# Border between projection and second attention: waiting for stored queries at each chunk's loads, and the first shift's store issued ahead of ones and x

## The reference, cut to what matters

```python
x = _layernorm(x + _L0_attn_ref(x, ...))           # ends with: return out @ proj_w.T + proj_b
x = _layernorm(x + _L0_xattn_ref(x, ctx_1024, ctx_1024, mask, ...))

def _L0_xattn_ref(q, k, v, mask, Wq, bq, Wk, bk, Wv, bv, Wo, bo):
    qh = _split_heads(q @ Wq.T + bq)
    kh = _split_heads(k @ Wk.T + bk)
    vh = _split_heads(v @ Wv.T + bv)
    scores = jnp.einsum('bhqd,bhkd->bhqk', qh, kh) / jnp.sqrt(jnp.float32(HEAD_DIM))
    scores = scores + mask.astype(scores.dtype) * NEG
    weights = jax.nn.softmax(scores, axis=-1)
    attn = jnp.einsum('bhqk,bhkd->bhqd', weights, vh)
```

## Time and profile before

| What | Value |
|---|---|
| Median of 3 runs | 1844.24 us |
| Lowest and highest run | 1839.27 and 1845.89 us |
| The profiled execution: its own time | 1838.95 us |
| The profiled execution: span | 1837.2 us |
| Mean granted TensorE clock | 0.927 of full speed |
| PE busy | 1628.8 us (89%) |
| DVE busy | 1281.4 us (70%) |
| ACT busy | 1010.5 us (55%) |
| POOL busy | 389.3 us (21%) |

### The profile page before, as it was taken

How to read it: one execution, slowest core, us unless ns; L and a number is a source line. 1 busy time by engine, 2 the same in 40 slices (tenths; PEclk the granted TensorE clock), 3 DMA queues, 4 the chain that set the end, 5 groups by cost and what they waited for, 6 DMA issues and landing times. The chain is left out here.

```text
span 1837.2 us, 36172 instructions
## 1 busy us (share of the span) xinstructions
PE 1628.8 (89%) x14816; PEld 1062.8 (58%) x14816; DVE 1281.4 (70%) x2240; ACT 1010.5 (55%) x1727; POOL 389.3 (21%) x265
## 2 busy tenths in 40 slices
PE   7859999999999999999877599869994999999990
PEld 7734444444444444444366455546763888888890
DVE  6978888888888888888178446752333678777744
ACT  5324777777777777777735267844542233333313
POOL 6550000000000000000015001111551355555521
PEclk9967999999999999999989678978996999999995
DMA  7887443433434333440248866223213244444226
GB/s 251 265 229 197 68 67 62 70 65 65 71 62 67 62 62 64 61 69 9 58 137 232 193 101 122 66 88 110 89 39 111 70 95 96 96 95 95 38 24 194
DMA packets 130388, 184.36 MB, mean 100 GB/s; under 512 B 29466, under 2 KB 93736, under 8 KB 129132
## 3 DMA queue, kind: packets, MB, share of 16 engines
q1 hardware_dynamic: 113456, 153.70, 35.5%
q0 software_dynamic: 13440, 22.07, 5.7%
q10 hardware_dynamic: 3328, 6.29, 2.1%
HBM read 115.32 MB, written 70.06 MB: 101 GB/s over the span
## 5 line engine op out<-in xcount | busy, mean ns | idle before, releaser
L719 DVE TENSOR_REDUCE att_row_max<-att_ring 128x2 f32<-128x1024 f32 x512 | 602.5, 1221 | 110.8 <-PE att_ring L785 57.1
L703 ACT ACTIVATE att_w_exp<-att_s_ps 128x512 f32<-128x512 f32 x999 | 536.2, 599 | 219.2 <-PE att_s_ps L832 146.8
L859 PE MATMUL att_a_ps<-att_w_exp,att_v_group 128*32 128x512 f32 x2048 | 272.8, 605 | 0.8 <-ACT att_acc_sb L692 0.6
L818 PE MATMUL att_s_ps<-att_q_stack,att_k_stack 62*128 62x512 f32 x640 | 181.8, 481 | 0.0
L818 PEld LDWEIGHTS att_s_ps<-att_q_stack,att_k_stack 62*128 62x128 f32 x640 | 84.4, 184 | 123.9 <-ACT att_w_exp L703 112.9
L2344 ACT ACTIVATE ex_hid<-ex_h_ps,ex_b 128x512 f32<-128x512 f32 x128 | 87.3, 686 | 118.5 <-DVE ex_h_lo L2399 64.9
L633 POOL COPY att_eyes<-keep_slope_eye 128x384 bf16<-128x384 bf16 x16 | 8.0, 506 | 634.7 <-PE att_s_ps L832 625.1
L2399 DVE TENSOR_TENSOR ex_h_lo<-ex_hid,ex_h_hi 128x512 fp32r<-128x512 f32 x128 | 138.7, 1084 | 4.4
L2294 POOL DMA_INDIRECT x_scr<-ex_y,ex_home x60 | 101.2, 1687 | 177.0 <-DVE ex_y L2389 163.3
L785 PE MATMUL att_ring<-att_k_stack,att_q_stack 60*128 60x512 f32 x640 | 131.5, 451 | 6.3 <-DVE att_att L746 3.2
L832 PE MATMUL att_s_ps<-att_eyes,keep_past_bf 64*128 64x64 bf16 x3738 | 130.7, 193 | 0.0
(11 more groups left out here) (314 smaller groups left out, 3567.6 us busy)
## 6 DMA issues: line engine op xcount, KB each, us to landing
first_w_raw<-ew SPq DMA_DIRECT2D x16, 1024.0 KB, 7.7
att_k_stack<-qk_scr SPq DMA_DIRECT2D x40, 256.0 KB
rows_scr<-att_zeros POOLq DMA_DIRECT2D x8, 1040.0 KB, 21.0
first_rows<-rows_scr SPq DMA_DIRECT2D x16, 520.0 KB, 4.8
qk_scr<-qkv_t_lo SPq DMA_DIRECT2D x14, 512.0 KB, 4.7
qk_scr<-qkv_t_hi SPq DMA_DIRECT2D x14, 512.0 KB, 4.4
keep_k_stack<-qk_scr SPq DMA_DIRECT2D x24, 256.0 KB
att_q_stack<-qk_scr SPq DMA_DIRECT2D x20, 256.0 KB
```

The costliest lines, as they stand in the source:

```text
L703: nc.scalar.activation(w_exp[(STEPS * g.n + st) % SETS][h][:, :], score_bank(v), ACT.Exp).then_inc(exp_done, 1)
L719: nc.vector.tensor_reduce(out, ring[place.slot][:, :, :], AX.X, ALU.max).then_inc(ring_free, 1)
L818: ins = nc.tensor.matmul(score_bank(v), ks[g.buf][rows, c, j, kt * P:(kt + 1) * P], qs[g.buf][rows, j, c * CH:(c + 1) * CH], start=True, s ...
L859: ins = nc.tensor.matmul(a_ps[32 * h:32 * h + 32, :], vg[g.buf][:, kt, h * VW:h * VW + 32], w_exp[(STEPS * g.n + st) % SETS][h][:, :], sta ...
```

## The change

The wait for the stored queries leaves the end of the projection's block. In its place, each load of a stack of queries waits for the stores of its own chunk, on SP and on ACT. DVE waits for all stores before it computes `wo_lo`, in the middle of the second attention's start. The semaphores `q_out` and the tiles `q_hi` and `q_lo` change their place of allocation for this: the semaphores outlive the stage, and the tiles stand behind the others. Apart from that, `move_top(0)` moves ahead of the ones of stacks 2 and 3 and of x1 of chunk 0.

```diff
@@ cross_tiles
-            "stacks": [s.sb(f"q_stack{i}", [P, PAIRS, CH], F32R) for i in range(2)]}
+            "stacks": [s.sb(f"q_stack{i}", [P, PAIRS, CH], F32R) for i in range(2)],
+            "q_out": [s.sem(f"q_out{i}") for i in range(2)]}
@@ stage_self_out
-        q_hi = [s.sb(f"q_hi{i}", [P, CK, CH], F32R) for i in range(2)]
-        q_lo = [s.sb(f"q_lo{i}", [P, CK, CH], F32R) for i in range(2)]
         norm = Norm(nc, s, io["apart"])
...
         wk_hi, wk_lo = [spare[:, i * 2048:(i + 1) * 2048].rearrange("p (c m) -> p c m", c=CK) for i in range(2)]
+
+        q_hi = [s.sb(f"q_hi{i}", [P, CK, CH], F32R) for i in range(2)]
+        q_lo = [s.sb(f"q_lo{i}", [P, CK, CH], F32R) for i in range(2)]
...
-        q_out = [s.sem(f"q_out{i}") for i in range(2)]
+        q_out = pre["q_out"]
...
             for c in range(2):
                 sp.wait_ge(x1_out[c], 16 * CHUNKS // 2)
-                sp.wait_ge(q_out[c], Q_STORES * CHUNKS // 2)
@@ stage_cross, SP
                 if n >= Q_SETS:
                     sp.wait_ge(s_done, H * (n - Q_SETS) + H)
+                sp.wait_ge(q_out[n % 2], Q_STORES * (n // 2 + 1))
                 load_query_side(sp, io, n, 0, qst[n % Q_SETS])
...
             load_stack(2)
+            move_top(0)
             for i in (2, 3):
                 load_ones(sp, io, qst[i], ones_in)
             load_x(0)
-            move_top(0)
             sp.dma_start(bo, io["bo"].partition_broadcast(P)).then_inc(weights_in, 16)
@@ stage_cross, ACT
+                act.wait_ge(q_out[n % 2], Q_STORES * (n // 2 + 1))
                 load_query_side(act, io, n, 1, qst[n % Q_SETS])
@@ stage_cross, DVE
+            for c in range(2):
+                dve.wait_ge(q_out[c], Q_STORES * CHUNKS // 2)
             dve.wait_ge(hi_done, 1)
             nc.vector.tensor_tensor(wo_lo[:, :, :], wo_raw, wo_hi[:, :, :].bitcast(F32), ALU.subtract).then_inc(lo_done, 1)
```

More of the change, by code:

```diff
@@ L1546, in stage_cross @@
         x2_done = s.sem("x2_done")
-        ones_in = lent["ones_in"]
+        ones_in, q_out = lent["ones_in"], pre["q_out"]
         out_done = s.sem("out_done")
```

## The result

| | Before | Changed |
|---|---|---|
| Median | 1843.20 us (20 runs) | 1834.88 us (20 runs) |
| Lowest and highest run | 1837.82 and 1857.50 us | 1830.36 and 1848.78 us |
| Profiled execution, own time / span | 1838.95 / 1837.2 us | 1835.53 / 1833.7 us |

The ratio of the changed kernel to the one before is 0.9955, with a 95% interval of 0.9938 to 0.9972: 8.3 us less, between 5.2 and 11.4. The forecast was 1834.8 us. The move is real, and its middle is just inside the half per cent.

A forecast was written before the change was run, and what follows sets the result against it. Two PE stalls at the border, 5.20 us (last query store landing) and 5.94 us (shift rows' load), were taken as the bound. Both parts -10.1, ones +0.7, sum -9.4: 1844.24 to 1834.8 us, range 1829.0 to 1841.0.

The forecast's parts named there:

- The border's wait: End of the projection: without the wait for stored queries the new stage begins at 1024.5 instead of 1029.14, 4.6 us saved.
- The added waits: SP and ACT at each stack load, DVE before wo_lo: stores will have landed by then, cost 0.
- The shift's store: First shift store, moved ahead: lands in 2.6 us instead of 8.1, PE's stall before first scores shrinks from 5.94 to 0.45.
- The ones: Ones moved behind the shift: PE waits 0.7 us for them at half 16, bounds no wait and 2.5 us.
- The second part of the change: Shift's store moved ahead of ones and x1: 5.5 us gained at chunk 0's first scores, 0.7 us lost at half 16.
- The sum: Whole kernel: -10.1 + 0.7 = -9.4 us, from 1844.24 to 1834.8 us.
- S: Issue time of the first shift's loads on SP: 1048.19 before, forecast at 1038.05 after the change.
- the cover of the second shift store: Chunk 1's first scores come 27.2 us after S, so a late second shift store is covered by some 5 us.
- Rival 1: Only the border is saved: shift's store still lands in 6.1 to 8.1 us, 1837.6 to 1839.6 us; chance 21%.
- rival 2: Something else holds the border's barrier until about 1029; only 4.8 us saved, 1839.4 us; chance 4%.
- Rival 3: Clock luck: the low-clock stretch in chunk 2 goes, -14.0 us, 1830.2 us; chance 14%.
- rival 4: Clock stays low in chunks 1 to 3: up to 14.8 us lost, +5.4, 1849.6 us; chance 5%.

The follow-up runs named there:

- e7: Changed kernel with SP waiting until all ones are in before it issues x1; one run, no median, PE's wait at half 16 was 4.09 us.
- e3: Changed kernel with the four ones issued ahead of the stack of chunk 2; 1835.32 us, ratio 0.9968 to the kernel before.
- e2: Kernel before with only the new order on SP, the old wait at the border kept; 1838.51 us, ratio 0.9983.
- g1: Kernel before with only the query tiles q_hi and q_lo allocated last; 1842.95 us, ratio 0.9997.
- g2: Repeat of g1, the kernel before with only q_hi and q_lo allocated last; one run, no median.
- f5: Changed kernel with chunk 2's two ones issued between the first shift's store and its wait, the other two later; 1832.21 us, ratio 0.9952 to the kernel before.
- f6: f5 with x1 of chunk 0 and bo moved behind chunk 1's shift; 1832.76 us, ratio 0.9961 to the kernel before.
- e1: Changed kernel with the old order on SP, ones and x1 ahead of the first shift's store; 1836.76 us, ratio 0.9973 to the kernel before.
- f7: Changed kernel with all four ones issued between the first shift's store and the wait for it; one run, no median, A + C 44.2 us.

## Why the prediction was right

**The border's wait** was forecast at 4.6 us. In the two profiles it is 5.23 - 0.56 = 4.7. Over all profiles that wait there A is 6.1 us in the mean (five of them), 0.56 in each that does not: 5.5 us. The profile I worked from had a short landing.

**The added waits** cost nothing, as forecast. DVE's `wo_lo` starts at 1037.70 in the changed kernel, between the maxima of halves 13 and 14 as before, and all query stores had landed at 1027.44. In the profile with the latest landing, e7, it was still 7 us ahead of `wo_lo` (1036.60 and 1043.76).

**The shift's store** was forecast to land in 2.6 us and did. First scores were to come 17.65 us after the first maxima, and came after 17.44 and 17.84. PE's wait was to be 0.45 us and is 0.25 and 0.66. The mechanism of that step was half wrong all the same: I took x1's common landing as the sign that bulk held the store; e3 shows that four ones ahead are enough, and both x1 and the store had their last four steps late behind the ones.

**The ones** are the term that was mis-sized. "I take 0.7 us" with 2.5 us as the bound; measured 4.68, 4.48 and, in e2, 4.60. The step that failed is the one from the pair of shift loads to four ones at "0.6 us more each". Seen from the end of their issue, the ones took 8.9 us and not 3.6 to 6.1. The second part of the change, forecast at 5.5 - 0.7 = 4.8 us, is worth about 1 us in e2 and nothing beside the new wait: the first scores do come 4 to 6 us sooner, and the wait at half 16 gives it back.

**The sum.** A + C falls from 48.8 us (mean of before, its repeat, g1 and g2) to 42.3 (mean of two), 6.5 us, inside the interval of 5.2 to 11.4 and 2.9 less than the forecast of 9.4. So the forecast's 1834.8 beside 1834.88 is closer than its working deserved, and that is luck: the ones took 4 us more, the border gave 1 us more, the forecast started from a median of 1844.24 us that 20 runs put at 1843.20, and the other 2 us of the measured 8.3 no run explains; they are within the interval.

**One count was wrong.** I put chunk 1's first scores of the kernel before at 1075.38; that is the second pair of chunk 1:

```profile
1072.03 0.69 PE L1811 MATMUL cr_score_ps<-pre_q_stack,pre_k_exp 50*77 50x512 f32 x2
...
1075.38 0.69 PE L1811 MATMUL cr_score_ps<-pre_q_stack,pre_k_exp 50*77 50x512 f32 x2
```

Chunk 0 has eight pairs, and 1072.03 is the ninth start of scores. It is 23.8 us after S, so the cover of the second shift store was 1.8 us and not 5. It landed in 10.3 us where I allowed 8.1, and no wait was recorded at 1063.39; in f5, f6 and e7 that cover is gone and PE waits 0.6, 1.6 and 0.9 us.

**The rivals.** Rival 1 (store still late) and rival 2 (something else holds the barrier) did not occur: 2.6 us, and A of 0.56 us. But what rival 1 said of the time, that only the border is saved, is what the ruler shows, for another reason: the stall moved from the first scores to half 16. Rival 3 and rival 4, the clock, show in single profiles, up to 14 us between them. Whether the clock moves the medians by a microsecond or two is not shown: the median granted clock of the runs is 0.928 in the changed kernel, 0.926 and 0.924 in runs of the kernel before beside the experiments, and 0.925 in e1, while 6.5 us less at 0.50 would by themselves raise it by 0.0015 (an estimate from A + C). The granted clock of chunk 1 is 0.78 in the kernel before, from its true start, and 0.79 in the changed one; that of chunk 2 is 0.73 and 0.81. Why the low stretches fall where they do stays open; no run was made for it.

## What to carry to other kernels

Here the wait for a store's landing at a barrier cost nearly the whole landing, 4.7 to 6.1 us, since nothing was left to compute; moved to the load that reads the data it cost nothing. When an urgent small transfer is moved ahead of others, the one next in need takes its place: look up when each of the moved ones is needed, and split off the part that is needed first. And take the cost of a border from several profiles: here it was 5.2 us in one and 6.0 to 6.7 in four.

## What the runs showed of the hardware that was not expected

A transfer of four rows of 16 KB is slow out of proportion to its 64 KB. Four of them, 256 KB, took 8.9 us from the end of their issue, while 1.5 MB of the stack, issued from 1021.68 on behind the tail of the stores, had landed at 1032.83, in 11.2 us. They also block: with them ahead a 64 KB store of 32 rows took 8.3 us against 2.2 to 2.6 without (e3 against e2, e7 and the changed kernel), and the two-row loads took 10.6 us to PE against 3.9 (f7 against the changed kernel).

The semaphore updates of the changed kernel's trace show how a transfer is divided. Each of the four ones raises its semaphore in five steps, one within 0.2 us of the end of its issue and four with its data, from 1039.60 to 1045.96 for all of them. A two-row load has three, one at once and two with its data. x1, with 128 rows, has sixteen: twelve between 1042.47 and 1043.28, four between 1047.75 and 1050.92. So a transfer of four rows has four parts that land on their own, and a transfer of sixteen parts that stands behind it has just four of them late, as in the kernel before and in e3.

The Trainium skill, in "DMA: Bandwidth & Descriptors", section "Why a DMA increments its semaphore by 16 and not by 1", says that the number of DMA engines a transfer is spread over is the largest number up to 16 that divides the sizes of both sides' slowest dimension of more than one element, and that a transfer issued as here takes the lowest-numbered ones. By that rule the ones run on four engines and the shift's loads on two of the same four. The trace agrees with the numbers: four and two late steps, and four of x1's sixteen held. Which engine carried which part the trace does not record, so that they are the same four is inferred, and loads with another outermost dimension were not tried.
